# Decoder layer with position-dependent attention: a second buffer for the queries, and the turns and scaled copies moved next to the two late sets

## What is computed

```python
q = x @ Wq
kv = x @ Wkv
k, v = jnp.split(kv, 2, axis=-1)
sim = jnp.einsum('bid,bjd->bij', q, k) * scale
sim = sim + _cope(q, sim, pos_emb)
attn = jax.nn.softmax(sim, axis=-1)
out = jnp.einsum('bij,bjd->bid', attn, v)
x = layernorm(x + out @ Wout + b_out)
x = layernorm(x + cross_attention(x, ctx_1024))
x = layernorm(x + low_rank_ffn(x))
```

## Time and profile before

| | |
|---|---|
| median of 3 runs | 2278.76 us (2276.46 to 2284.88) |
| profiled execution, its own time | 2286.39 us |
| profiled execution, span | 2284.3 us |
| mean granted clock of TensorE | 0.990 of full speed |
| PE, ACT, DVE, POOL busy | 96%, 77%, 71%, 17% of the span |
| logits of the 128 attention bodies | from 34.6 to 1835.4 us of the span |

### The profile page before, as it was taken

The page is one execution under the profiler, slowest core; times in us unless marked ns, Lnnn a source line. Parts: engine busy times, 40 slices in busy tenths (PEclk is TensorE's granted clock), DMA queues, the critical chain, the costliest instruction groups (busy, mean ns, idle before and its releaser), DMA issues. The chain is left out here.

```text
span 2284.3 us, 53247 instructions
## 1 busy us (share of the span) xinstructions
PE 2191.0 (96%) x14577; PEld 1487.9 (65%) x14577; DVE 1633.2 (71%) x4269; ACT 1752.7 (77%) x3723; POOL 389.5 (17%) x673
## 2 busy tenths in 40 slices
PE   7999999999999999999999999999998979999997
PEld 5666666666666666666666666666665557777775
DVE  5888888888888888888888888888888811323231
ACT  5888888888888888888888888888888843454543
POOL 1111111111111111111111111111111101212121
PEclk9999999999999999999999999999999989999997
DMA  2010101010101010101010101010001021010100
GB/s 65 24 32 25 30 24 30 24 30 26 30 25 31 23 30 24 30 24 30 24 30 24 30 24 30 24 31 25 24 15 48 13 67 35 30 39 30 39 30 7
DMA packets 107087, 67.04 MB, mean 29 GB/s; under 512 B 27821, under 2 KB 104814, under 8 KB 106990
## 3 DMA queue, kind: packets, MB, share of 16 engines
q1 hardware_dynamic: 106990, 65.56, 10.7%
HBM read 14.33 MB, written 2.10 MB: 7 GB/s over the span
## 5 line engine op out<-in xcount | busy, mean ns | idle before, releaser
L843 DVE TENSOR_REDUCE mx<-Sc 128x1 f32<-128x1024 f32 (+1 forms) x512 | 564.6, 1128 | 225.9 <-PE Sc L632 225.9
L482 ACT ACTIVATE probsT<-rings 128x512 f32<-128x512 f32 x1024 | 542.6, 601 | 180.9 <-PE rings L640 180.8
L506 ACT ACTIVATE probs<-Sc,nbias 128x1024 f32<-128x1024 f32 x512 | 568.8, 1125 | 28.1 <-DVE nbias L853 28.0
L640 PEld LDWEIGHTS rings<-ident,probs 128*128 128x128 f32 x4096 | 447.3, 143 | 203.2 <-issue 122.4
L640 PE MATMUL rings<-ident,probs 128*128 128x128 f32 x4096 | 530.8, 278 | 2.2 <-ACT probs L506 2.2
L632 PE MATMUL Sc<-qk,q_now 64*128 64x512 f32 x2048 | 506.6, 607 | 26.5 <-ACT probs L506 12.5
L654 PE MATMUL out<-probsT,V 128*64 128x256 f32 x4096 | 498.3, 384 | 19.0 <-issue 9.8
L654 PEld LDWEIGHTS out<-probsT,V 128*64 128x64 f32 x4096 | 311.8, 136 | 140.6 <-issue 65.9
L806 DVE COPY_PREDICATED z<-mask,z 128x224 f32<-128x224 int16 (+5 forms) x768 | 394.6, 514 | 11.3
L374 POOL TENSOR_TENSOR prod<-cut,z 128x350 f32<-128x350 f32 x128 | 120.5, 941 | 1460.0 <-DVE z L818 1460.0
L632 PEld LDWEIGHTS Sc<-qk,q_now 64*128 64x128 f32 x2048 | 182.6, 186 | 186.3 <-issue 172.1
(11 more groups left out here) (128 smaller groups left out, 2292.0 us busy)
## 6 DMA issues: line engine op xcount, KB each, us to landing
q_now<-qk SPq DMA_DIRECT2D x256, 64.0 KB, 2.0
xv<-xT SPq DMA_DIRECT2D x113, 128.0 KB, 2.2
q_far<-qk SPq DMA_DIRECT2D x256, 32.0 KB, 1.8
at<-attn SPq DMA_DIRECT2D x16, 512.0 KB, 3.2
probs<-in_x_dram SPq DMA_DIRECT2D x4, 512.0 KB, 5.6
wqk<-in_L_attn_Wq_dram SPq DMA_DIRECT2D x32, 64.0 KB, 2.1
xin<-in_x_dram SPq DMA_DIRECT2D x16, 128.0 KB, 2.8
out_dram<-res SPq DMA_DIRECT2D x16, 128.0 KB, 1.7
```

The source lines that it names most:

```text
L482: nc.scalar.activation(probsT[:, u, 4 * s:4 * s + 4, :], ring[SLOT_BANK[k]][:, :].rearrange("p (t q) -> p t q", q=P), ACT.Copy).then_inc(s ...
L506: nc.scalar.activation(probs[:, u, cols], Sc[:, cols], ACT.Exp, bias=nbias[:, u:u + 1], accum_out=sums[:, u, half:half + 1]).then_inc(exp_ ...
L640: last = nc.tensor.transpose(ring[SLOT_BANK[k]][:, j * P:(j + 1) * P], probs[:, u, (4 * s + j) * P:(4 * s + j + 1) * P], ident[:, :])
L843: nc.vector.tensor_reduce(mx[:, u, half:half + 1], Sc[:, cols], AX.X, ALU.max).then_inc(dve_unit, 1)
```

## The change

`q_now` gets two buffers, chosen by the parity of the body. `load_now(g + 1)` moves from behind the far load to the start of SP's body, where it waits until the logits of body g - 1 are done (`bank_full` at 4g) and until its predecessor has landed (`now_in`). On PE `turns_of(g - 2)` moves from between the second and third of the last sets to a place right behind the two late sets. On ACT the two scaled copies move in the same way: behind the two late sets, ahead of all four last sets.

```diff
-        q_now = sb("q_now", [P, 2 * P])
+        q_now = sb("q_now", [P, 2, 2 * P])
...
             def load_now(g, odd):
                 h, t = g // PAIRS, g % PAIRS
-                sp.dma_start(q_now[0:C, :], queries(h, odd, t)).then_inc(now_in, 16)
-                sp.dma_start(q_now[C:P, :], queries(h, odd, t)).then_inc(now_in, 16)
+                for r in range(2):
+                    sp.dma_start(q_now[r * C:(r + 1) * C, int(odd), :], queries(h, odd, t)).then_inc(now_in, 16)
...
-            def body(g, odd, late=False, first=False, tile=True, far=True, near=False):
+            def body(g, odd, late=False, first=False, tile=True, far=True, now=True, near=False):
                 base = slots_before(g, late)
+                if now:
+
+                    if not first:
+                        wait_apart(sp, bank_full, g * 4, waited)
+                    wait_apart(sp, now_in, g * 32 + 32, waited)
+                    load_now(g + 1, not odd)
                 if far:
...
-                wait_apart(sp, bank_full, g * 4 + 4, waited)
-                load_now(g + 1, not odd)
                 if tile:
...
                     transposed(0, base, at.late, (2, 3))
-                    transposed(1, base, at.last, (0, 1))
                     if not second:
                         scale(g - 2, 0)
                         scale(g - 2, 1)
-                    transposed(1, base, at.last, (2, 3))
+                    transposed(1, base, at.last)
...
-            def logits(par, u, half):
+            def logits(par, odd, u, half):
...
                     transposes(0, base, at.late, 2, late_before)
                     transposes(0, base, at.late, 3, late_before)
+                    if not second:
+                        turns_of(g - 2)
                     transposes(1, base, at.last, 0, late_before)
                     transposes(1, base, at.last, 1)
-                    if not second:
-                        turns_of(g - 2)
                     transposes(1, base, at.last, 2)
                     transposes(1, base, at.last, 3)
                     outputs(g - 1, base, at.last, range(EARLY_TILES), keys, empty=not second)
```

More of the change, by code:

```diff
@@ L631, in logits @@
                     bank = half * 2 + r
-                    last = nc.tensor.matmul(Sc[:, bank * BANK:(bank + 1) * BANK], q_now[rows, u * P:(u + 1) * P],
+                    last = nc.tensor.matmul(Sc[:, bank * BANK:(bank + 1) * BANK], q_now[rows, int(odd), u * P:(u + 1) * P],
                                             qk[rows, par, r, cols], start=True, stop=True)
@@ L675, in body @@
                     wait_apart(pe, exp_done, g * 4 - 1, waited)
-                logits(par, 0, 0)
+                logits(par, odd, 0, 0)
                 if not first:
@@ L680, in body @@
                     wait_apart(pe, slot_out, base - 1, waited)
-                logits(par, 0, 1)
+                logits(par, odd, 0, 1)
                 if not first:
@@ L695, in body @@
                 wait_apart(pe, exp_done, g * 4 + 1, waited)
-                logits(par, 1, 0)
+                logits(par, odd, 1, 0)
                 wait_apart(pe, exp_done, g * 4 + 2, waited)
-                logits(par, 1, 1)
+                logits(par, odd, 1, 1)
                 transposes(0, base, at.now, 0)
@@ L738, in _ @@
             transposes(0, base, at.late, 3, late_before)
+            turns_of(G - 2)
             transposes(1, base, at.last, 0, late_before)
             transposes(1, base, at.last, 1)
-            turns_of(G - 2)
             transposes(1, base, at.last, 2)
```

## The result

| | before | after |
|---|---|---|
| median | 2279.95 us (2276.46 to 2284.88, 5 runs) | 2293.72 us (2292.11 to 2346.75, 5 runs) |
| profiled execution, its own time | 2286.39 us | 2292.34 us |
| profiled execution, span | 2284.3 us | 2290.5 us |

The change makes the kernel slower by a little: 1.0056 times the time of before, 95% interval 1.0042 to 1.0070. The forecast was 2289.7 us. One of the five runs, the one of 2346.75 us, was disturbed and is not in the ratio.

The account below looks back on a forecast made before the run. The prediction took PE's fixed order, busy 98% of the main loop, to set the pace. From the median, 2278.8 - 5 (late loads) + 3.3 (moved loads) + 12.6 (freed bank) = 2289.7 us, range 2271 to 2298 us.

Parts of the forecast that it names:

- The freed bank: PE's fourth last set waits for the bank ACT's copy frees; `outputs` 0.10 us later in 126 bodies, 12.6 us more.
- The late loads: Waits of `logits` for `q_now` vanish with two buffers: 8.6 us less profiled, 5 us less in the median run.
- The moved loads on SP: Query loads ahead of the far load on SP's queue delay `q_far` by 1.5 us; 3.3 us more in all.
- Between heads: After a change of head, slow far-load landings show in four of 13 bodies, a third of a microsecond each: 1.3 us.
- Body 0: PE already waits 2.05 us for `q_far` in body 0; the two issues come on top: 1.2 us more.
- Body 120: PE already waits 0.99 us for `q_far` in body 120; 0.8 us more, backlog of data rather than issue setting the landing.
- That PE's work is unchanged and so the period: Rival: exchanging work within PE, busy 98% of the loop, gives nothing; 2277 us, chance 0.22.
- That the wait for the scaled copies goes and none comes: Rival: `outputs` start up to 0.08 to 0.16 us sooner over 126 bodies; about 2262 us, chance 0.10.
- The late far load: Rival: SP's delay exceeds 2.1 us, so PE waits in all 13 bodies after a change of head; 2295 us, chance 0.06.

Follow-up runs that it names:

- Experiment 2: Kernel of before with only the turns and scaled copies moved as in the change, one query buffer and old load order: 2295.64 us, ratio 1.0061.
- Experiment 6: Kernel of before with only ACT's scaled copies moved behind the two late sets, PE's turns left in place, one query buffer: 2410.64 us, ratio 1.0565.
- Experiment 3: Kernel of before with two query buffers and load_now issued early but behind the far load, PE and ACT order kept: 2276.33 us, ratio 0.9971.
- experiment 7: Kernel of before with the edits of Experiment 3 and experiment 5 together: 2247.65 us, ratio 0.9853.
- experiment 5: Kernel of before with PE's turns behind the two late sets, ACT's scaled copies between first and second last sets, one query buffer: 2257.33 us, ratio 0.9894.
- Experiment 1: Kernel of before with only the loads' half of the change: two query buffers, load_now ahead of the far load: 2280.37 us, ratio 0.9989.
- run 126: Not a follow-up run: part of the words "run 126 times", the count of bodies with turns in one execution.

## Why the prediction was right, and where its sizes were off

To put sizes on its terms I cut every body of both traces at the logits of unit 1. The first part, from the body's first logits, holds the turns and the far load, and sums to 16.6 us more than before; the second part, up to the next body's first logits, holds the late loads and sums to 10.3 us less. From the first part come 13.6 us for the turns, 2.4 for the far load and 0.6 of body 0, which its second part gives back. So the terms were 13.6, 2.4 and -9.7 us, sum +6.3, where the prediction had 12.6, 3.3 and -8.6, sum +7.3.

**The freed bank** was the step that decided, and it was right in kind and in size. Scaled copies were put at 1.90 us and came at 1.91, `outputs` at 3.56 and 3.52 and came at 3.55 and 3.52, the stand of PE ahead of the last four transposes at about 0.3 and was 0.32 and 0.35. Averaged over the 126 bodies with turns, from the records of the two traces, `outputs` moved from 3.43 to 3.53 us, 0.104 a body. Experiment 2 has it alone at 13.9 (11.2 to 16.7). Experiment 6 confirms the coupling itself: 0.41 + 0.61 + 0.64 us from the scaled copy to `outputs`.

**The late loads** were right in the profiled execution: 8.6 us forecast, 9.7 measured. The three waits that the view put down to an exponential are gone with the others, so they were late loads, as the prediction read them. For the runs without the profiler I took 5 us out of 1 to 8.6. Experiment 3 against before gives 6.6 us (4.1 to 9.1), which doesn't exclude 5, and experiment 7 against 5 gives 9.7 by the medians. The term was probably too small, by 2 to 5 us: the five profiled executions with one buffer have 5.1 to 9.7 us of late loads (experiment 7). So the 7.6 us between the profiled execution and the median are at most in part late loads.

**The moved loads on SP** came out near the forecast in the sum (2.4 us, forecast 3.3) and not in its parts; that the sum is so near is luck.
- Between heads I had 1.3 us in four bodies, and it was 2.05 in four: 0.73, 0.48 and 0.49 us in bodies 64, 72 and 80, and 0.35 in body 16. The delay of the far load is 1.8 us and not 1.5. The slow landings were foreseen; the slow issues of weights ahead of it in the queue, which make it late in bodies 64 and 72, were not.
- Body 0: I had 1.2 us. The wait did grow as said, from 2.05 to 3.30, but nothing of it reaches the end in this execution. The failed step of this term is that I charged it without looking what stands behind it. PE in body 0, before and then after, from the first logits to those of the next body (lines of the timelines):

```profile
34.63 1.99 PE L632 MATMUL Sc<-qk,q_now 64*128 64x512 f32 x8 [0.56 <-ACT V L424]
...
39.85 3.37 PE L632 MATMUL Sc<-qk,q_now 64*128 64x512 f32 x8 [0.52 <-ACT probs L506]
...
46.36 1.13 PE L632 MATMUL Sc<-qk,q_now 64*128 64x512 f32 x4 [0.80 <-ACT probs L506]
```

```profile
34.28 1.99 PE L634 MATMUL Sc<-qk,q_now 64*128 64x512 f32 x8 [0.56 <-ACT V L428]
39.57 0.47 PE L608 MATMUL rings<-qk,q_far 64*128 64x240 f32 x1 [3.30 <-DMA q_far<-qk]
...
40.08 1.88 PE L634 MATMUL Sc<-qk,q_now 64*128 64x512 f32 x8
...
46.01 1.13 PE L634 MATMUL Sc<-qk,q_now 64*128 64x512 f32 x4 [1.71 <-issue]
```

  From 34.63 to 46.36 before, and from 34.28 to 46.01 after, it is 11.73 us both times. The late window has room because PE isn't what the body waits for: DVE comes to the row maxima of unit 1 7.72 us after the first logits in both traces, and finds the logits that it reads done both times. How much room there is depends on the clock. Before, the logits of unit 1 take 3.37 us, with a granted clock of 0.50 from 40 to 42 us; after, they start 0.6 us later in the body and take 1.88 at full clock. Experiment 1 has the same order on SP, but a granted clock of 0.50 from 40 to 46 us, and the logits take long and start late:

```profile
40.92 3.62 PE L636 MATMUL Sc<-qk,q_now 64*128 64x512 f32 x8
```

  DVE waits for them there, and the body takes 13.45 us, 1.7 more than before. So body 0 costs nothing in one trace with this order and 1.7 us in the other. Why the clock fell in one and not in the other isn't shown; PE had stood for 3.3 us in both.
- Body 120: 0.99 became 1.36 us, 0.4 instead of 0.8. The far load was issued 1.74 us later and landed 0.49 us later, so here, as the prediction had it, the issue alone doesn't set the landing.

Experiments 1 and 3 price the whole queue order: 4.0 us by the medians.

**The sum.** Forecast for the profiled execution 2293.7 us, measured 2292.34; for the median 2289.7, measured 2293.72. The first is 1.4 too high: 1.0 by the three terms, and the first logits come 0.34 us sooner after than before. The second is 4.0 too low; 1.2 of it is the median of before, which was 2278.76 then and 2279.95 now. The rest is not told from nothing by runs of this number: the ratio gives 9.6 to 16.0 us, and the forecast was 2289.7 - 2278.8 = 10.9.

**The rivals.** That PE's work is unchanged and so the period would have given 2277 us: refuted by experiment 2, and again by experiment 5, which has the same work and takes 24 us less. That the wait for the scaled copies goes and none comes was given 2262 us, and its condition was a delay below 0.3 us behind the turns. The delay was 0.42 us in odd and 0.38 in even bodies, so it did not come to pass, and in the two bodies with a shorter delay the change costs time as well (last section). Experiment 5 shows that what it would bring is there to be had, by another order. The late far load at 2295 us lies near the measured time, and its condition, over 2.1 us of delay, was met in bodies 64 and 72; but experiment 1 shows that the time isn't from there.

## What to carry to other kernels

When two engines pass banks round a ring, an instruction moved ahead on the consumer delays every bank whose copy it passes: follow the bank that is needed soonest, from its release to the work that waits for it, and put other work behind its copy (experiment 5), neither ahead of it nor two copies later. A wait of 0.1 us in a body that is run 126 times is worth more than a transfer that is late by a whole microsecond in ten bodies. And when a load gets a second buffer, leave it in the queue behind what is needed sooner; it gains from the earlier permission, not from the earlier place.

## What the runs showed of the hardware

- From the end of the turns to the scaled copy it is 0.42 us in body 73, after as before, and 0.41 in experiment 6, even though ACT stands idle there. In bodies 126 and 127, which are written out and not part of a loop on ACT, it is less. The timelines in body 127, PE then ACT after, and PE before:

```profile
1833.91 1.09 PE L642 MATMUL rings<-ident,probs 128*128 128x128 f32 x8
1834.85 0.56 PE L665 MATMUL out<-fold,halves 128*128 128x64 f32 x4
...
1837.22 2.81 PE L656 MATMUL out<-probsT,V 128*64 128x256 f32 x24
...
1835.58 0.52 ACT L496 ACTIVATE attn<-out,rsum 128x64 f32<-128x64 f32 x2
```

```profile
1828.02 2.00 PE L640 MATMUL rings<-ident,probs 128*128 128x128 f32 x16
...
1831.28 2.81 PE L654 MATMUL out<-probsT,V 128*64 128x256 f32 x24
```

- A wait may hide in a busy column: PE's busy time rose by 12.06 us with the same instructions.
- Issues and landings vary. The far load lands 1.7 us after its issue at the least, 1.8 at the median and 3.3 at the most, and the last load of weights between heads took 0.37 us to issue in most bodies and 1.26 and 1.48 in two. A margin of 0.4 us was not enough in four of thirteen bodies.
